# Constant rows of the second stack on SyncE's queue, and six of the eight products of o_w with w1 made while the first stack is loading

## What is computed

```python
x = x + 0.5 * ffn(layernorm(x))
x = x + attention(layernorm(x))
x = x + 0.5 * ffn(layernorm(x))

def ffn(hs):                                  # H = 16 heads, KPH = 8, E = 8 experts, top 2
    Q, K, V = hs @ q_w + q_b, hs @ k_w + k_b, hs @ v_w + v_b
    attn = softmax(Q[..., :KPH] @ K.T / sqrt(KPH))
    mla_out = concat(attn @ V, 0) @ o_w + o_b
    probs = softmax(mla_out @ router_w + router_b)
    combine = weights of the two largest probs, normalised
    h1 = gelu(mla_out @ w1[e] + b1[e])        # w1: (E, 256, 512)
    return hs + 0.3 * sum_e combine[e] * (h1 @ w2[e] + b2[e])
```

## Time and profile before

| | |
|---|---|
| median of 3 runs | 2160.52 us (2152.19 to 2161.12) |
| the profiled execution | 2161.11 us |
| its span, first to last instruction | 2159.4 us |
| TensorE busy | 1849.6 us (86%) |
| VectorE busy | 1539.8 us (71%) |
| ScalarE busy | 926.3 us (43%) |
| GpSimd busy | 603.3 us (28%) |
| granted TensorE clock, mean | 0.927 of full speed |

### The profile page before, as it was taken

How to read it: one execution, slowest core, us unless ns; L and a number is a source line. 1 busy time by engine, 2 the same in 40 slices (tenths; PEclk the granted TensorE clock), 3 DMA queues, 4 the chain that set the end, 5 groups by cost and what they waited for, 6 DMA issues and landing times. The chain is left out here.

```text
span 2159.4 us, 38745 instructions
## 1 busy us (share of the span) xinstructions
PE 1849.6 (86%) x12392; PEld 1025.5 (47%) x12392; DVE 1539.8 (71%) x3941; ACT 926.3 (43%) x1694; POOL 603.3 (28%) x789
## 2 busy tenths in 40 slices
PE   1799999999949995999999983699999999769991
PEld 1443333333348883566666662133333332258880
DVE  2578888888456664788888763678898889346665
ACT  0136666666712222444444421056666666612220
POOL 2212333231236663000000001222233331246660
PEclk9789999999969997999999986589999999879995
DMA  8335333331022224111110005336333321023227
GB/s 200 62 48 124 75 75 65 64 62 29 22 68 71 71 71 146 40 41 40 41 41 11 11 11 114 68 65 137 65 67 65 73 53 23 29 90 120 81 70 243
DMA packets 146419, 154.12 MB, mean 71 GB/s; under 512 B 18828, under 2 KB 134540, under 8 KB 145868
## 3 DMA queue, kind: packets, MB, share of 16 engines
q1 hardware_dynamic: 118880, 104.35, 21.6%
q0 software_dynamic: 12928, 34.49, 4.8%
q10 hardware_dynamic: 14412, 12.79, 2.8%
HBM read 86.75 MB, written 58.34 MB: 67 GB/s over the span
## 5 line engine op out<-in xcount | busy, mean ns | idle before, releaser
L602 DVE TENSOR_REDUCE f_M<-bank 128x1 f32<-128x512 f32 x1024 | 672.7, 685 | 184.3 <-PE bank L885 174.2
L510 ACT ACTIVATE f_PT<-bank 128x512 f32<-128x512 f32 x1024 | 566.0, 607 | 264.8 <-PE bank L904 260.0
L885 PE MATMUL bank<-f_KS,f_QS 96*128 96x512 bf16 x1024 | 405.8, 403 | 59.0 <-DVE f_M L602 27.1
L904 PE MATMUL bank<-f_QS,f_KS 99*128 99x512 bf16 x1024 | 383.6, 387 | 27.5 <-ACT f_PT L510 16.8
L904 PEld LDWEIGHTS bank<-f_QS,f_KS 99*128 99x128 bf16 x1024 | 100.0, 100 | 390.6 <-ACT f_PT L510 276.7
L914 PE MATMUL bank<-f_PT,f_V 128*32 128x512 f32 x2048 | 273.8, 605 | 0.0
L885 PEld LDWEIGHTS bank<-f_KS,f_QS 96*128 96x128 bf16 x1024 | 101.9, 100 | 179.6 <-DVE f_M L602 109.5
L1146 PE MATMUL bank<-f_room,f1m_gT 128*128 x568 | 137.4, 386 | 0.1
L1146 PE MATMUL bank<-f_room,f2m_gT 128*128 x568 | 136.2, 383 | 0.3
L439 POOL DMA_INDIRECT routed_rows<-f_AO,f_rows_i x128 | 123.6, 965 | 42.1 <-issue 42.1
L1084 ACT ACTIVATE f2m_gT<-f2m_hb 128x512 f32<-128x512 f32 x71 | 44.7, 630 | 161.1 <-DVE f2m_hb L1108 158.8
(11 more groups left out here) (256 smaller groups left out, 3058.2 us busy)
## 6 DMA issues: line engine op xcount, KB each, us to landing
f_QS<-q_parts SPq DMA_DIRECT2D x192, 64.0 KB
f_KS<-k_parts SPq DMA_DIRECT2D x168, 64.0 KB
xr<-f_xr SPq DMA_DIRECT2D x16, 512.0 KB, 3.2
f_room<-in_L_ffn_w SPq DMA_DIRECT2D x2, 4096.0 KB, 22.6
fc_rows<-expert_rows SPq DMA_DIRECT2D x16, 512.0 KB, 10.9
la_rows<-expert_rows POOLq DMA_DIRECT2D x14, 512.0 KB, 5.1
q_parts<-f_q SPq DMA_DIRECT2D x16, 384.0 KB, 2.5
k_parts<-f_k SPq DMA_DIRECT2D x16, 384.0 KB, 2.5
```

Source lines behind the costliest of these rows:

```text
L510: act.activation(PT[:, i % 8, :], score_bank(e, i)[:, :], ACT.Exp).then_inc(probs_ready, 1)
L602: dve.tensor_reduce(M[:, t, h:h + 1], SCM[(a * SC + i) % 3][:, :], AX.X, ALU.max).then_inc(scm_drained, 1)
L885: pe.matmul(SCM[(a * SC + i) % 3][:, :], QS[par][0:K_MAX, h, t * P:(t + 1) * P], KS[par][0:K_MAX, h, :], start=True, stop=True).then_inc(s ...
L904: pe.matmul(score_bank(a, i)[:, :], KS[par][0:K_EXP, h, t * P:(t + 1) * P], QS[par][0:K_EXP, h, :], start=True, stop=True).then_inc(sce_fi ...
```

## The change

On SyncE and ScalarE: the three DMAs of a stack's constant rows become a function; ScalarE calls it for the first unit's stack at its start, SyncE for the other stack after it has issued the loads of the first unit's stack. This holds in both passes. In the first pass, TensorE makes the products of o_w with w1 for experts 0 to 5 in `begin_folds`, between the evacuation of the transposed o_w and the router's small products, before turn one; groups 0 and 2 of turn one make those of experts 6 and 7. ScalarE evacuates o_w and products 0 and 1 before it issues the K loads of the first stack, and products 2 to 5 after. The bias products stay where they are.

```diff
@@ -133,6 +133,7 @@
     PV_S = PV_W // 2
     GROUPS = SC // HQ
     G_LAST, G_FIRST = 0, 12
+    FOLDS_FIRST, FOLDS_EARLY = 2, 6
     SCORE_SCALE = 1.0 / float(np.sqrt(KPH))
     OUT_SCALE = 0.5 * 0.3
     START, END = nth * B, (nth + 1) * B
@@ -320,6 +321,16 @@
                 at = eng.value_load(pad_i[0:1, e:e + 1], min_val=0, max_val=xs.shape[0] - P)
                 eng.dma_start(xs[ds(at, P), :], zero_rows[:, e, :]).then_inc(pads_stored, 16)
 
+        def fill_constant_rows(eng, i):
+
+            rows = slice(K_TERMS, K_MAX)
+            for to in (QS[i], KS[i]):
+                eng.dma_start(to[rows, :, :], zero_b[rows, :].unsqueeze(1).to_broadcast([K_MAX - K_TERMS, H, S])) \
+                   .then_inc(constant_rows[i], 16)
+            eng.dma_start(KS[i][K_MAX:K_EXP, :, :].rearrange("p h (x y) -> p (h x) y", y=P),
+                          w["ones_b"][K_MAX:K_EXP, :].unsqueeze(1).to_broadcast([PARTS, H * S // P, P])) \
+               .then_inc(constant_rows[i], 16)
+
         @block.sync
         def _(sp):
             def load(a):
@@ -379,7 +390,11 @@
                     sp.wait_ge(small_filled, 1)
                 load_w2(sp)
 
-            run_turns(sp, turn, after_third=fetch_w2)
+            def fill_second_stack():
+                sp.wait_ge(init, INIT)
+                fill_constant_rows(sp, (START + 1) % 2)
+
+            run_turns(sp, turn, after_first=fill_second_stack, after_third=fetch_w2)
             sp.wait_ge(pads_ready, nth + 1)
             store_pads(sp, 0)
 
@@ -512,8 +527,8 @@
                         root(f)
                     if f is not None and g in FRONT:
                         FRONT[g](f)
-                    if fold is not None and e is None and s is not None and g % 2 == 0:
-                        evacuate_fold(g // 2)
+                    if fold is not None and e is None and s is not None and g % 2 == 0 and FOLDS_EARLY + g // 2 < E:
+                        evacuate_fold(FOLDS_EARLY + g // 2)
                     if p is not None and g in POST:
                         POST[g](p)
                     if e is not None and g == HH:
@@ -522,6 +537,11 @@
                     pv_out(e, 1)
 
             def begin_folds():
+                if fold is not None:
+                    act.wait_ge(owT_filled, 1)
+                    act.activation(fold["owT"][:, :, :].rearrange("p c k -> p (c k)"), SCE[0][:, 0:D], ACT.Copy).then_inc(owT_ready, 1)
+                    for e in range(FOLDS_FIRST):
+                        evacuate_fold(e)
 
                 act.wait_ge(split_stored, START * 32 + 32)
                 for half in range(HALVES):
@@ -530,8 +550,8 @@
                         act.dma_start(KS[START % 2][n * KPH:(n + 1) * KPH, heads, :],
                                       k_scr[j].rearrange("(h k) t -> k h t", k=KPH)[:, heads, :]).then_inc(half_loaded[half], 16)
                 if fold is not None:
-                    act.wait_ge(owT_filled, 1)
-                    act.activation(fold["owT"][:, :, :].rearrange("p c k -> p (c k)"), SCE[0][:, 0:D], ACT.Copy).then_inc(owT_ready, 1)
+                    for e in range(FOLDS_FIRST, FOLDS_EARLY):
+                        evacuate_fold(e)
 
             def evacuate_fold(e):
                 act.wait_ge(fold_filled, e + 1)
@@ -544,14 +564,7 @@
 
             act.preload_act_table_set(LN_TABLE)
             act.wait_ge(init, INIT)
-            for i in range(2):
-                for to in (QS[i], KS[i]):
-                    rows = slice(K_TERMS, K_MAX)
-                    act.dma_start(to[rows, :, :], zero_b[rows, :].unsqueeze(1).to_broadcast([K_MAX - K_TERMS, H, S])) \
-                       .then_inc(constant_rows[i], 16)
-                act.dma_start(KS[i][K_MAX:K_EXP, :, :].rearrange("p h (x y) -> p (h x) y", y=P),
-                              w["ones_b"][K_MAX:K_EXP, :].unsqueeze(1).to_broadcast([PARTS, H * S // P, P])) \
-                   .then_inc(constant_rows[i], 16)
+            fill_constant_rows(act, START % 2)
             run_turns(act, turn, after_first=begin_folds, after_second=end_folds)
             act.wait_ge(pads_ready, nth + 1)
             store_pads(act, 1)
@@ -929,7 +942,10 @@
                         if f is not None and g in FRONT:
                             FRONT[g](f, i % HQ)
                     if fold is not None and e is None and s is not None:
-                        (fold_weight, fold_bias)[g % 2](g // 2)
+                        if g % 2 == 1:
+                            fold_bias(g // 2)
+                        elif FOLDS_EARLY + g // 2 < E:
+                            fold_weight(FOLDS_EARLY + g // 2)
                     if e is not None and g == G_LAST + 3:
 
                         pe.wait_ge(v_ready, min(e + 2, END) if isinstance(e, int) else e + 2)
@@ -955,6 +971,8 @@
                     last = pe.transpose(SCE[0][:, c * P:(c + 1) * P], w["o_w"][:, c * P:(c + 1) * P], ident[:, :])
                 last.then_inc(owT_filled, 1)
                 pe.wait_ge(owT_ready, 1)
+                for e in range(FOLDS_EARLY):
+                    fold_weight(e)
                 pe.wait_ge(wide_ready, 1)
                 for at, left in ((0, fold["owT"]), (E, fold["o_b_wide"])):
                     for c in range(DC):
```

## The result

The changed kernel took 2145.60 us, the median of 10 runs (2140.42 to 2148.76); the kernel before, in 10 runs beside it, 2159.94 us (2150.98 to 2162.51). The ratio is 0.994 with a 95% interval of 0.9927 to 0.9953: 0.6% faster, 14 us. The profiled execution took 2143.63 us (span 2141.9), 17.5 us less than the profiled one of before.

What follows compares the result with a forecast made beforehand. Bound by the wait for ScalarE's root in both openings, and in turn one by TensorE, with VectorE waiting behind it. 2161.1 − 14.8 + 0 + 2.5 = 2148.8, forecast 2149 us; range 2134 to 2159.

Steps and rivals of the forecast that it cites:

- Term 1: Openings of both passes: ScalarE takes the variance's root earlier, without three DMA issues before it; −9 and −5.8 us.
- q10's 21.1%: First opening: ScalarE's DMA queue, carrying second-stack constant rows, took 21.1% of the engines' time from 24 to 49.5 us.
- Rival (d): First opening: other transfers, not the issue, set the first stack's time; the first pass gains nothing; 2158 us, chance 0.05.
- Term 2: Constant rows issued behind the stack loads on SyncE hold it ten us or more but delay nothing; taken at nothing.
- Rival (c): Both openings: constant rows run beside the first stack's loads, not behind, and delay them; 2165 us, chance 0.08.
- Term 3: First opening: six big products fit in before the first stack arrives; taken 0, bounds 0 to +4 us.
- Rival (b): First opening: the first products hold up the first stack; +4 us, 2153 us, chance 0.12.
- Term 4: Turn one without six big products: the low clock makes the remaining small products dearer; +2.5 us, bounds −10.5 to +8.
- the argument on the clock: Turn one, groups 8 to 13: at the low clock sixteen bias products take 3.8 us; three pairs gain only 0.5 us.
- Rival (a): Turn one: the clock stays up, or the turn is not sensitive to it; 2137 us, chance 0.22.

Runs made afterwards that it cites:

- its quarter: The kernel before with four bias products an expert instead of sixteen, the rest left out, all big products still in turn one: 2147.88 us, one run.
- before, once more: The kernel before, unaltered, run again for a second profile: 2155.57 us, one run.
- changed, once more: The changed kernel, unaltered, run again for a second profile: 2143.83 us, one run.

## Why the prediction was right, point by point

**Term 1 was right in both passes**: −9 taken, −8.97 measured; −5.8 taken, −5.75 measured. The root came at 17.75 and 1310.89, right behind the variance. The argument from q10's 21.1% held: the queues' own work, not only the issue, let the store of the parts land at 40.59 (forecast 41). The −9 itself was a choice between two bounds, 6.8 and 10.4, so that it fell within 0.1 us is partly luck. Rival (d) is out. The times that the prediction named for the second pass (root 1324, K loads 1343, first score 1357) leave out what the first pass would have gained; by its own sum (−9 + 2.5) they should have read 1317, 1337 and 1351. Measured were 1310.89, 1330.29 and 1346.28, the first two a further 6 us earlier, since turn one became 4 us shorter in that execution and not 2.5 longer.

The Trainium skill, "DMA: Bandwidth & Descriptors", section "Issuing engines are not separate DMA queues", adds that the issue time saved by another issuer is "usually small relative to the DMA itself". Here it was not: one issue of 768 KB held SyncE for 5.47 and in the second pass 8.75 us, that of 48 KB behind it 7.2 us, where the packets of a block of 768 KB kept the 16 DMA engines for some 4.5 us (an estimate: its share of the 3.13 MB that took 90.6% of 20 us); and the sequencer's time is the whole −5.8 of the second pass. The measurement decides.

**Term 2 held.** SyncE stood in its issues for 13.6 us, more than the ten named, and nothing that anyone waited for was behind it. Rival (c) is out: the first stack took 15.6 us (15.4 before), and the rows held back until it had landed gained nothing. The second stack took 14.0 us in the three profiles of before and its quarter, and 14.7 to 16.0 in the eight with rows issued beside it (three of them 15.8 to 16.0). The products alone, with the rows still on ScalarE, took 14.5, and the rows held back 14.95, so 1 to 1.5 us at most can be laid to the rows beside it.

**Term 3 held, with more cover than thought.** The forecast was products 0 and 1 evacuated at 40.8; it was 36.3, as the first four products ran at 1.8 us each, right behind the projections, and not at 3.6 (16 instructions in 7.13 us). The router's products ended at 52.4, not 55.0, and the stack came at 56.18 (56.4). The cover was 3.8 us, not 1.4. Rival (b) is out.

**Term 4: the mechanism right, the sizes off in places, the sum within what one turn varies.** Going by the same points in each turn (the first maxima of groups 8 and 12, the first score of the next turn), in us:

| kernel | to group 8 | groups 8 to 11 | from group 12 | sum |
|---|---|---|---|---|
| before | 34.9 | 16.3 | 17.0 | 68.2 |
| before, once more | 33.1 | 15.9 | 17.8 | 66.8 |
| changed | 30.9 | 14.9 | 18.4 | 64.2 |
| changed, once more | 34.7 | 14.9 | 19.7 | 69.2 |

Groups 8 to 11 are where the argument on the clock was made. The bias products doubled (3.41; forecast 3.8), VectorE waited 2.56 behind them (2.9), and a pair took 7.44 us (7.9): it exchanged two waits, of 2.0 to 2.75 behind the product and of 0.6 to 1.0 behind the bias products, for one. From group 12 on the changed kernel lost 0.6 to 2.6 us, where the V projections and the last bias products ran at the low clock, as forecast (the projections' sixteen instructions took 4.2 us in place of 2.4). The part that was mis-sized is the beginning: +0.8, +0.2 and +0.4 were taken for groups 4 to 6, and up to group 8 it came out at −4.0 in one execution and −0.2 in the other, against the first profile of before. The two executions reach the bias products of group 5 after 20.8 and 21.2 us and those of group 7 after 28.8 and 32.5: what lies between is whether the clock rises before group 5's bias products or behind them. The prediction treated this as a property of the kernel; the two executions show that it is one of the execution. Its bounds (−10.5 to +8) held all of it.

Rival (a), that the clock stays up, is out by the rows of the turn (0.68, 0.62), although 64.2 alone could have been taken for half of it. By the medians the products alone are worth +0.11% (−0.02 to +0.25), 2.4 us; the prediction took +2.5. That the two agree to 0.1 us is luck: the interval goes from −0.4 to +5.4 us, and the prediction's own bounds were 18.5 us apart. What is sound is the sign of the argument, that the clock would take back what the idle times promised: 10.5 us of waits went, and nothing was gained.

**What was missed** is a cause, not a time. The prediction saw the low clock as the price of a thinner turn and asked only what the bias products would cost when it fell, not what they cost already: 15.1 of the 64.93 us that TensorE works in the turn of before. The kernels with a quarter of them show it. With eight big products the turn falls from 68.1 us (mean of three) to 54.9, with two from 67.6 (mean of four) to 56.6: 13 and 11 us for the bias products, and for six big ones 0.5 us with the bias products there and −1.7 with a quarter of them, both less than two executions of one kernel differ. With the big products in the turn, cutting the bias products saves their time and raises the clock; with the big ones gone, it saves their doubled time at the low clock. The Trainium skill, "TensorE: Matmul & The Clock Gate", section "What's actually happening", has the half-rate clock as the default that activity lifts; the trace agrees where the big products go (0.68 against 0.77), but the rule alone would not have said that the clock rises when the bias products go, which is less work too (0.90 against 0.77). And the prediction's step from that rule, that a turn with thinner work can be no shorter, did not hold: 54.9 us against 68.2.

**What stays open.** Why, with the same instructions, the clock rises before group 5's bias products in one execution and after them in the next; how the 13 us divide between the bias products' own time (11.1 us of TensorE's busy time) and the clock (5.9 us of the big products'), since busy times overlap and no run changed one without the other; and whether the second stack's 14.7 to 16.0 us, against 14.0 before, is the rows' doing or spread.

## What to carry to other kernels

When a step is moved out of a stretch that TensorE and VectorE share, ask of each part both what it costs the busier engine and whether the clock falls when it goes: here the many one-column products were the ones to move, and the dense products could stay. DMA issues in front of a critical instruction cost the time that they hold the engine's queue, which the timeline shows as idle time that ends with "issue"; here they were the whole gain, and they were long only behind other transfers issued just before them on the same queue. And when a term of the sum hangs on the clock, read the stretch in more than one profiled execution before believing a difference of some us.

## What the runs showed of the hardware

- Sixteen products of one column with full weights took 1.84 us (0.115 each) at a granted clock of 1.00 and 3.41 us (0.213 each) at 0.50; nothing in between but in sets during which the clock rose or fell (1.95 to 2.17).
- Dense work can lift the clock and still not pay: eight added products of 512 columns in each of six groups brought it to 0.72 over the turn, from 0.60 to 0.68 in four executions without them, and made most of the bias products cheap; the turn was 73.1 us, longer than without them (64.2 to 70.6).
- The same DMA issue held its engine for very different times: a block of 768 KB for 0.64 to 0.79 us as the first or second of its kind, and for 4.3 to 8.8 us when some 1.5 MB had been issued on the same queue just before it; one of 48 KB for 1.3 to 7.2 us.
- Two executions of one kernel differed by 5.0 us in one turn of 64 to 69 us, with VectorE's work equal (46.83 and 46.84 us) and the clock at 0.68 and 0.62, and yet by 0.2 us in the whole (2143.63 and 2143.83): other stretches gave it back, the second stack 1.1 us of it and the turn behind it 2.5.
